# A sandwich of attention and a gated FFN on one core: the third score block moved behind the first pair of the FFN's last layer in TensorE's loop

## The reference

```python
x = x + layernorm(attention(layernorm(x)))
x = x + layernorm(ffn(layernorm(x)))

def attention(x, w_lhs, w_rhs):            # one head of width 128, softmax over 512
    scores = einsum('nsd,ntd->nst', x * w_lhs, x * w_rhs)
    return einsum('nst,ntd->nsd', softmax(scores, axis=2), x)

def ffn(x, ...):                           # 128 -> 512 -> 512 -> 512 -> 128, ternary weights
    h = silu((x @ w1) * s1) * ((x @ w2) * s2)
    h = gelu((h @ h1) * s_h1)
    h = gelu((h @ h2) * s_h2)
    return (h @ w3) * s3
```

## Time and profile before

| what | value |
|---|---|
| median of 3 runs | 508.02 us (507.04 to 508.2) |
| the profiled execution's own time | 508.16 us |
| its span, first to last instruction | 506.4 us |
| outside the span | 1.8 us |
| granted clock of TensorE over the span | 0.991 |
| PE busy | 486.3 us, 96% |
| ACT busy | 447.9 us, 88% |
| DVE busy | 394.4 us, 78% |
| POOL busy | 228.8 us, 45% |
| DMA | 24.23 MB, mean 48 GB/s |

### The profile page before, as it was taken

The page is one execution under the profiler, slowest core; times in us unless marked ns, Lnnn a source line. Parts: engine busy times, 40 slices in busy tenths (PEclk is TensorE's granted clock), DMA queues, the critical chain, the costliest instruction groups (busy, mean ns, idle before and its releaser), DMA issues.

```text
span 506.4 us, 9435 instructions
## 1 busy us (share of the span) xinstructions
PE 486.3 (96%) x2850; PEld 387.8 (77%) x2850; DVE 394.4 (78%) x1178; ACT 447.9 (88%) x750; POOL 228.8 (45%) x249
## 2 busy tenths in 40 slices
PE   7889999999999999999999999999999999999993
PEld 6677778787887878778787878778787887787771
DVE  5999889696968969696896969789695778666564
ACT  5989898999989899998989998999998999886862
POOL 3366744545254454525445452433626234133620
PEclk9989999999999999999999999999999999999997
DMA  7122010111203020110303011010220101100112
GB/s 272 42 85 62 2 62 2 51 55 39 65 0 104 0 69 34 41 63 0 104 0 97 7 41 62 1 62 3 63 83 1 62 3 63 42 1 1 41 64 65
DMA packets 12989, 24.23 MB, mean 48 GB/s; under 512 B 1568, under 2 KB 2080, under 8 KB 12960
## 3 DMA queue, kind: packets, MB, share of 16 engines
q1 hardware_dynamic: 12960, 23.87, 14.6%
HBM read 15.48 MB, written 8.39 MB: 47 GB/s over the span
## 4 chain that ended last, share of the span: by engine, by line
PE 70%; ACT 13%; DVE 11%; issue 4%; DMA 1%; POOL 0%; POOLq 0%; DVEq 0%; ACTq 0%
PE hid_bank L350 19%; PE hid_bank L352 18%; PE score_bank L299 4%; ACT hC_full L1174 3%; PE hid_bank L371 3%; PE score_bank L318 3%; PE mix_bank L340 2%; PE hid_bank L375 2%; PE mix_bank L336 2%; PE hid_bank L376 2%; PE hid_bank L372 2%; PE w_bank L308 2%; PE mix_bank L337 2%; PE w_bank L352 2%; PE score_bank L321 2%
## 5 line engine op out<-in xcount | busy, mean ns | idle before, releaser
L350 PE MATMUL hid_bank<-hA_hi,w_hi 128*128 128x512 f32 x256 | 106.5, 416 | 0.2 <-DVE hA_full L1513 0.2
L350 PE MATMUL hid_bank<-hB_hi,w_hi 128*128 128x512 f32 x256 | 104.0, 406 | 1.3 <-DVE hB_lo L1606 1.2
L352 PE MATMUL hid_bank<-hB_lo,w_hi 128*128 128x512 f32 x256 | 101.4, 396 | 0.1
L352 PE MATMUL hid_bank<-hA_lo,w_hi 128*128 128x512 f32 x256 | 101.1, 395 | 0.0
L2067 POOL TENSOR_TENSOR hC_lo<-hC_full,hC_hi 128x512 fp32r<-128x512 f32 x60 | 76.4, 1293 | 30.0 <-ACT hC_full L1174 29.9
L1513 DVE SCALAR_TENSOR_TENSOR hA_full<-hid_bank,columns,gate 128x512 f32<-128x512 f32 x64 | 46.6, 746 | 24.6 <-ACT gate L1167 24.6
L1598 DVE TENSOR_TENSOR eT_lo<-score_bank,eT_hi 128x512 f16<-128x512 f32 x56 | 38.0, 679 | 31.7 <-ACT eT_hi L1148 31.7
L350 PEld LDWEIGHTS hid_bank<-hB_hi,w_hi 128*128 128x128 f32 x256 | 48.2, 188 | 13.0 <-DVE hB_lo L1606 3.3
L352 PEld LDWEIGHTS hid_bank<-hB_lo,w_hi 128*128 128x128 f32 x256 | 48.3, 189 | 10.7 <-DVE hB_lo L1606 1.2
L350 PEld LDWEIGHTS hid_bank<-hA_hi,w_hi 128*128 128x128 f32 x256 | 48.3, 189 | 9.5 <-DVE hA_full L1513 1.1
L352 PEld LDWEIGHTS hid_bank<-hA_lo,w_hi 128*128 128x128 f32 x256 | 48.4, 189 | 8.4
(11 more groups left out here) (111 smaller groups left out, 1229.7 us busy)
## 6 DMA issues: line engine op xcount, KB each, us to landing
x_res<-x_dram SPq DMA_DIRECT2D x16, 256.0 KB, 2.7
out_dram<-x SPq DMA_DIRECT2D x16, 256.0 KB, 2.0
x_tail<-out_dram SPq DMA_DIRECT2D x16, 256.0 KB, 2.9
x_in<-x_dram SPq DMA_DIRECT2D x15, 256.0 KB, 2.8
out_dram<-y_out SPq DMA_DIRECT2D x15, 256.0 KB, 3.0
w_raw<-weights_dram SPq DMA_DIRECT2D x5, 512.0 KB, 5.3
x_ahead<-x_dram SPq DMA_DIRECT2D x1, 256.0 KB, 4.5
w_raw<-weights_dram SPq DMA_DIRECT2D x1, 256.0 KB, 5.8
```

Of the source, the lines that this page charges most:

```text
L350: nc.tensor.matmul(bank[:, :], w_hi[:, w], hi, start=first, stop=False)
L352: mm = nc.tensor.matmul(bank[:, :], w_hi[:, w], lo, start=False, stop=last and not general)
```

## The change

Inside `step` two lines (the wait and score block 2) move behind two others (the wait and the first pair of layer 3). Start, finish and the other engines stay as they are, and no instruction is added or removed.

```diff
                     layer2(general, back4, 3, 3)
+                    pe.wait_ge(x2T_lo_ready, back4 + 2)
+                    layer3(general, back4, 0)
                     pe.wait_ge(e_lo_ready, back1 * T + 1)
                     scores(back1, 2)
-                    pe.wait_ge(x2T_lo_ready, back4 + 2)
-                    layer3(general, back4, 0)
                     pe.wait_ge(gelu2_done, back3 * K - 2)
                     gated(general, back3, 0)
```

## The result

| | before | changed |
|---|---|---|
| median | 508.02 us (507.04 to 508.95, 5 runs) | 511.62 us (510.74 to 512.58, 5 runs) |
| ratio to before | | 1.007, 95% interval 1.005 to 1.009 |
| span of the profiled execution | 506.4 us | 509.8 us |
| a loop step, mean of seven periods | 29.47 us | 29.91 us |

The kernel is 3.6 us slower; 511.9 was forecast, in a range from 510.4 to 513.3. The interval does not hold 1.

A forecast was written before the change was run, and what follows sets the result against it. PE, busy 96%, was taken as the bound. 0.59 - 0.11 = 0.48 us a step, times 8 = 3.8 us, took the profiled 508.16 to 512.0; 0.14 less for the median gave 511.9 us, range 510.4 to 513.3.

The forecast's parts named there:

- The wait that comes first: After layer 2, PE now meets the wait for `x2T_lo` before layer 3: 0.74 us instead of 0.14.
- Gated block 0 later by 0.59: In each step PE reaches gated block 0 at 213.11 instead of 212.52, 0.59 us later.
- What is given back: At gated block 2 `hA_full` stays put, PE's wait goes and the weight load is hidden: 0.11 us back per step.
- DVE's margin: Before `hA_full`, DVE's `att_n` would end at 215.28, still 0.13 us before `hA_full` starts at 215.41.
- PE's own lateness: At gated block 2 PE comes 0.59 us late, so even 0.4 more on DVE would not hold it up.
- The sum: Over the loop: 0.59 less 0.11 is 0.48 us a step, times 8 is 3.8 us slower.
- The lower bound of the sum: If PE could start layer 3 with DVE's end, 0.06 earlier: 8 x 0.42 = 3.4 us, 511.4 us.
- the forecast's own range: Whole-kernel time of 511.2 to 512.7 us, said to lie wholly above the 0.3% that counts as no change.
- The finish: After the loop: old order kept, and engines enter it with the same offsets, so no change in its time.
- The delay was not swallowed: Rival, chance 0.06: `hA_full` sets the pace at gated block 2, so PE's delay costs nothing; 508 us.
- The clock stayed: Rival, chance 0.02, said the clock falls through PE's idle of some 0.7 us in every step; about 525 us.

The follow-up runs named there:

- e1: Kernel before, old matmul order, with only the wait for `x2T_lo` moved ahead of score block 2: 512.24 us, ratio 1.0085.
- e3: Kernel before, with x2T's two copies put ahead of those of the score transpose on ACT and DVE: 511.93 us, ratio 1.0073.
- e4: Kernel before, with the last product of layer 2's block 0 issued two pairs sooner: 505.61 us, ratio 0.9952.
- e6: Changed kernel, with score block 2 four matmuls later still, behind gated block 0: 513.64 us, ratio 1.0110 to the kernel before.
- e2: Changed kernel, with x2T's two copies ahead of those of the score transpose: 508.74 us, ratio 1.0013 to the kernel before.
- e7: Changed kernel, with x2T's copies ahead of the score transpose's and layer 2 block 0's last product two pairs sooner: 505.05 us.
- e5: Changed kernel, with the last product of layer 2's block 0 two pairs sooner: 508.8 us, ratio 1.0015 to the kernel before.

## Why the prediction was right

*The wait that comes first.* `x2T_lo` was to end 0.91 us after the start of layer 2's last matmul, in the same place as before, and it ends at 0.92 in both kernels. PE was to start at 0.97, and does: 0.96 to 0.99 in the eight steps. e1 and e3 show that this alone makes the price.

*Gated block 0 later by 0.59.* Measured: from 1.64 to 2.23.

*What is given back.* 0.11 was reckoned for the hidden weight load at gated block 2. The lead of before shrinks from 0.57 there to 0.46 at gated block 3: 0.11. The 0.02 between 0.59 and 0.57 is the small wait at gated block 2 (0.01 in the working, which I named but did not subtract) and 0.01 that is lost on the way there. e4 and e6 move the same load from late to hidden and back.

*DVE's margin.* 0.13 was reckoned, 0.14 is seen between the rows, and e6 shows that the real room was 0.22, for the working had left out the overlap of DVE's rows; the error was on the safe side. The sentence that PE's own lateness would cover another 0.4 holds too: in e6 `hA_full` is 0.70 later than in the change, and only 0.14 of that becomes a wait, with 0.10 for the load.

*The sum.* 0.48 us a step was forecast, 0.43 measured (29.91 less 29.47), 3.5 us in the loop against 3.8. Beyond gated block 3 the difference goes from 0.46 to 0.43; the cause of those last hundredths is open. The medians differ by 3.6. The lower bound of the sum was 511.4, while the paragraph on the chances calls the forecast's own range 511.2 to 512.7; nothing hangs on the 0.2. The finish is unchanged to within 0.3 us, as assumed: from the first transpose of `turn_y` in the last step to PE's last matmul it is 190.98 us in the changed kernel, 190.97 to 191.16 in the seven experiments, and 191.25 in the trace of the kernel before.

*The profiled executions* agree with the sum in part by luck. Their spans differ by 3.4 us, but they are not eight times 0.43. The last matmul of layer 2 in the first step stands at 92.98 before and 93.42 after, and anywhere from 92.45 to 93.92 in the nine traces, though no kernel edits the start: that is 0.44 of the 3.4. The seven periods give 3.0. And from the last matmul of layer 2 in the last step to the end of the span it is 207.08 us before and 207.06 after, although this stretch holds the eighth step's delay (`turn_y` starts 8.42 after that matmul and not 7.98): the trace of the kernel before happens to be slower by 0.3 from there to the last matmul and by 0.2 behind it, where the nine traces scatter from 7.67 to 8.39 us. Spans of single executions are not to be subtracted for tenths; periods are.

*The rivals.* The delay was not swallowed (the wait at gated block 2 was 0.01 us, and e1 and e3 pay the full price as well). The clock stayed: the stretch from 94 to 330 us has a granted clock of 1.00 although PE is held up by 0.73 to 0.76 us in every step.

```profile
94.00:330.00 236.00, 231.41 (x1394) 188.70 (x1395) 191.23 (x583) 216.96 (x362) 109.35 (x121) 1.00 0.14 45
```

The Trainium skill, TensorE: Matmul & The Clock Gate, section "A second HAM failure mode: psum-queue depth-cycling", says that short idles between groups of matmuls, if frequent enough, make the clock swing. One such idle a step does not do it here.

In the loops of the nine traces 80 matmuls of 512 columns were released by a wait that held their weight load too. Each has the load at its own start, and the next matmul follows 0.33 to 0.35 us later. The Trainium skill, TensorE: Matmul & The Clock Gate, section "Step-by-step: what each phase is for", has weight loads pulled ahead of matmuls in flight; over a semaphore wait that does not happen in these traces, as the sum had taken it.

## What to carry to other kernels

When a block is moved on a saturated engine, ask what it had been covering: here three matmuls of 0.7 us in all covered most of the second of two copies. Whatever stands first on PE should need the copy that is made first. There are two remedies. One is to keep both orders alike (e2, e7). The other is to start the whole chain sooner by the one product that it hangs on, which gained 2.6 us on the kernel before (e4) and 2.8 us on the changed one (e5) without touching the place where the wait was seen. A second wait further on changes what the first is worth: in e2 PE comes 0.16 us later to gated block 0, and only 0.03 later to gated block 3. So both have to be followed.

## What the runs showed of the hardware that was not expected

A wait of a few hundredths costs more than itself. In e2 the score block is held up by 0.03 us (0.26 in place of 0.23), and its second matmul then comes 0.34 us later, so 0.11 more is paid; and a wait that ends just inside the preceding matmul, as at gated block 2 of the kernel before (0.01 us), costs the 0.10 to 0.11 all the same. At score block 2, layer 3 and gated block 2 of all nine traces the load starts 0.05 us after the row that releases it has ended, if the matmul ahead has started by then. How much of the load is hidden depends on how long before the matmul's start that row ended:

| releasing row ends before the matmul by | where | next matmul follows after |
|---|---|---|
| 0.05 to 0.06 us | the 80 late loads | 0.33 to 0.35 us |
| 0.13 | score block 2 in three steps of e7 | 0.26 to 0.27 |
| 0.14 to 0.15 | one step of e7, three of e4 (gated block 2) | 0.24 to 0.25 |
| 0.16 to 0.19 | gated block 2, all steps of e2 | 0.23 to 0.24 |

So here 0.16 us was enough to hide the load in full.
